# A latent-attention block on one core: four more products in three rounded passes, inverse square roots by one GpSimd power

## The reference

```
x = x + xattn(layernorm(x), ctx)      # q and k are normalised per head of 16 numbers, then softmax(q k) v
x = x + attn(layernorm(x))            # scores = QK/4 + lambda * (tanh(Q) J) tanh(K), causal
h = layernorm(x)
x = x + shared(h) + sum over the two best experts of prob * expert(h)
# shared(h) = (silu(h @ gate) * (h @ up)) @ down ;  router = softmax(h @ router_w)
```

## Time and profile before

| | us |
|---|---|
| median of 3 runs | 1395.9 |
| profiled execution | 1382.5 |
| its span, first to last instruction | 1380.7 |
| TensorE busy in the span (matmuls) | 1240.6 (90%) |
| VectorE busy | 984.4 (71%) |
| ScalarE busy | 698.1 (51%) |
| GpSimd busy | 450.4 (33%) |

### The profile page before, as it was taken

The page is one execution under the profiler, slowest core; times in us unless marked ns, Lnnn a source line. Parts: engine busy times, 40 slices in busy tenths (PEclk is TensorE's granted clock), DMA queues, the critical chain, the costliest instruction groups (busy, mean ns, idle before and its releaser), DMA issues.

```text
span 1380.7 us, 54869 instructions
## 1 busy us (share of the span) xinstructions
PE 1240.6 (90%) x22808; PEld 1024.0 (74%) x22808; DVE 984.4 (71%) x2498; ACT 698.1 (51%) x1377; POOL 450.4 (33%) x436
## 2 busy tenths in 40 slices
PE   3789999999999999999999999999999986699950
PEld 3677878888888878788878787888888864488840
DVE  7458777777777777777777777777777763365547
ACT  1345555555555555555555555555555542255520
POOL 1322333333333333333333333333333222155530
PEclk7789999999999999999999999999999998699985
DMA  4100111111111111103111100111111002586558
GB/s 155 39 21 4 48 49 49 49 49 49 49 49 51 56 44 51 34 30 100 33 34 33 36 29 28 34 33 34 34 38 33 15 14 63 157 245 188 163 188 262
DMA packets 82579, 92.12 MB, mean 67 GB/s; under 512 B 17248, under 2 KB 72544, under 8 KB 82016
## 3 DMA queue, kind: packets, MB, share of 16 engines
q1 hardware_dynamic: 70816, 65.41, 16.4%
q0 software_dynamic: 6912, 19.01, 3.8%
q10 hardware_dynamic: 4608, 4.20, 0.9%
HBM read 61.19 MB, written 33.78 MB: 69 GB/s over the span
## 4 chain that ended last, share of the span: by engine, by line
PE 82%; DVE 9%; issue 4%; DMA 2%; ACT 1%; POOL 1%; SPq 0%; DVEq 0%; POOLq 0%; ACTq 0%
PE ringB L489 16%; PE ringC L500 14%; PE oA L582 10%; PE banksS L565 9%; DVE mx L1220 6%; PE banksS L783 5%; PE banksS L529 4%; PE ringB L663 3%; PE ringB L617 2%; PE ringB L649 2%; PE banksS L634 2%; PE ringB L484 2%; DMA out<-ksq 2%; PE oA L489 2%; PE banksS L544 2%
## 5 line engine op out<-in xcount | busy, mean ns | idle before, releaser
L863 ACT ACTIVATE pt<-banksS 128x1024 f32<-128x1024 f32 x128 | 127.7, 1023 | 129.6 <-PE banksS L565 118.0
L1039 POOL TENSOR_TENSOR kn<-kc,rr 128x512 f32<-128x512 f32 x64 | 66.6, 1062 | 336.0 <-DVE rr L1208 336.0
L500 PE MATMUL ringC<-wx_kv,ct 128*128 128x256 f32 x512 | 159.9, 312 | 13.6 <-DVE ws_down L1362 6.2
L1220 DVE TENSOR_REDUCE mx<-banksS 128x8 f32<-128x2048 f32 x64 | 146.3, 2287 | 0.9 <-PE banksS L544 0.9
L500 PE MATMUL ringC<-wx_kv_rest,ct 128*128 128x256 f32 x512 | 146.8, 287 | 0.0
L500 PE MATMUL ringC<-wx_kv,ct_rest 128*128 128x256 f32 x512 | 146.0, 285 | 0.0
L1033 POOL TENSOR_TENSOR sc<-sc,rz 128x1024 f32<-128x1024 f32 x32 | 62.3, 1948 | 223.5 <-DVE rz L1281 223.5
L565 PE MATMUL banksS<-qT,kT 17*128 17x64 f32 x4096 | 132.4, 278 | 0.9 <-DVE qT L1225 0.9
L565 PEld LDWEIGHTS banksS<-qT,kT 17*128 17x128 f32 x4096 | 123.5, 191 | 7.9 <-issue 1.4
L500 PEld LDWEIGHTS ringC<-wx_kv,ct 128*128 128x128 f32 x512 | 99.3, 194 | 27.6 <-DVE pos_u L1338 7.8
L1234 DVE RECIPROCAL rz<-oA 128x128 f32<-128x128 f32 x64 | 61.3, 957 | 55.5 <-PE oA L582 55.5
(11 more groups left out here) (219 smaller groups left out, 2957.0 us busy)
## 6 DMA issues: line engine op xcount, KB each, us to landing
ct_in<-in_ctxT SPq DMA_DIRECT2D x64, 256.0 KB, 3.1
pt<-rows_by_expert SPq DMA_DIRECT2D x80, 130.0 KB, 2.4
rows_by_expert<-in_pad_rows SPq DMA_DIRECT2D x16, 260.0 KB
xt<-in_x SPq DMA_DIRECT2D x32, 128.0 KB, 3.5
rows_without_experts<-base SPq DMA_DIRECT2D x32, 128.0 KB
pt<-expert_rows SPq DMA_DIRECT2D x16, 256.0 KB, 4.1
kn<-expert_rows SPq DMA_DIRECT2D x16, 256.0 KB, 4.2
out<-ksq ACTq DMA_DIRECT2D x32, 128.0 KB, 3.8
```

The lines of the kernel that those rows point to most:

```text
L500: mm = pe.matmul(ringC[:, half * DIM:(half + 1) * DIM], left[:, p, k, j // 2, (j % 2) * P:(j % 2 + 1) * P], right[:, k, part * DIM:(part + ...
L863: act.activation(pt[:, g, :, :, :, :].rearrange("p i q c n -> p i (q c n)"), banksS[:, :, g * 256:(g + 1) * 256], ACT.Exp)\
L1039: pool.tensor_tensor(kn[:, 2 * jj:2 * jj + 2, :, 0:HD].rearrange("p j h d -> p (j h) d"), kc[:, 2 * jj:2 * jj + 2, :].rearrange("p j (h d) ...
L1220: dve.tensor_reduce(mx[:, 2 * r:2 * r + 2, :, HD].rearrange("p q i -> p i q"), banksS[:, :, :].rearrange("p i (q m) -> p i q m", q=2), AX. ...
```

## The change

1. QK, VP, ROUTE and GU become `split_product`: six rounded passes for each. ScalarE's copies of x1T and hT now round (`rounded["NT"]`, `rounded["HT"]`), and VectorE subtracts the rounded rows from the bank to get the rest (`self_rows_rest`, `ffn_rows_rest`), which is also what frees the bank. The weights are loaded into buffers that self attention uses later (sc, qkn, qk4) and are split on VectorE once, in step 3, where the scaling of jmix and ws_down now stands too (before: step 2).
2. The first guess and the Newton steps go; VectorE only makes mean plus epsilon (`mean_squares`), and GpSimd raises 80 columns to the power -0.5 in front of the key scaling.
3. Orders: TensorE turns x1n in front of rough_scores 0 instead of behind it; VectorE's keys 0 stand at the end of a step instead of the start of the next, ScalarE's probs_in 1 likewise; the two subtractions get places.
4. Room: w_down gets no buffer of its own but lies over kn and kT; its four loads are issued after the last tile's C1, its scaling stands in step 36 instead of 34, the w_gu loads come in steps 6 to 13, and the last pass uses other buffers.

```diff
+            def split_product(bank_, u, t, left, left_rest, source, right, right_rest, n):
+                pe.wait_ge(rounded[source].sem, rounded[source].of(t))
+                for r in (right, right_rest):
+                    for k in range(KD):
+                        pe.matmul(bank_[:, 0:n], left[:, k, :], r[:, k, 0:n], start=(r is right and k == 0), stop=False)
+                pe.wait_ge(free[source].sem, free[source].of(t))
+                for k in range(KD):
+                    mm = pe.matmul(bank_[:, 0:n], left_rest[:, k, :], right[:, k, 0:n], start=False, stop=(k == 1))
+                mm.then_inc(full[u].sem, 1)
...
             def self_qk(b, p):
                 if b == 0:
                     pe.wait_ge(self_weights_in, 16 * 7)
+                    pe.wait_ge(weights_set, 2)
                 claim(pe, B_USES, B_BANKS, "QK", b)
-                pe.wait_ge(free["NT"].sem, free["NT"].of(b))
-                product(bankB("QK"), "QK", lambda k: x1T[:, k, :], wa_qk, 2 * DIM)
+                split_product(bankB("QK"), "QK", b, x1T, x1T_rest, "NT", wa_qk, wa_qk_rest, 2 * DIM)
...
             def step(s, odd):
+                on(s, odd, 4, self_rows_turned)
                 on(s, odd, 3, rough_scores, 0)
-                on(s, odd, 4, self_rows_turned)
...
+            def inverse_sigmas(c, p):
+                pool.wait_ge(ev["s_eps"].sem, ev["s_eps"].of(c))
+                freed(pool, ev["qn_ready"], c)
+                pool.tensor_tensor(rr[:, :], ss[:, :], minushalf[:, :].to_broadcast([P, 5 * H]), ALU.pow).then_inc(ev["sigmas_ready"].sem, 1)
...
-            def inverse_sigmas(a, p):
+            def mean_squares(a, p):
 
                 for s in ("q_sum", "k_sum0", "k_sum1"):
                     dve.wait_ge(ev[s].sem, ev[s].of(a))
                 dve.tensor_scalar(ss[:, :], ss[:, :], 1.0 / HD, EPS, ALU.mult, ALU.add).then_inc(ev["s_eps"].sem, 1)
...
-                for n in range(3):
...
+            def self_rows_rest(b, p):
+                dve.wait_ge(rounded["NT"].sem, rounded["NT"].of(b))
+                freed(dve, full["QK"], b)
+                freed(dve, full["VP"], b)
+                dve.tensor_tensor(x1T_rest[:, :, :].rearrange("p k n -> p (k n)"), bankB("NT")[:, 0:DIM],
+                                  x1T[:, :, :].rearrange("p k n -> p (k n)").bitcast(F32), ALU.subtract).then_inc(free["NT"].sem, 1)
...
             def step(s, odd):
-                if s == TILES + 2:
+                if s == TILES + 4:
                     dve.wait_ge(expert_weights_in, 16 * 12)
                     dve.tensor_scalar(w_down[:, :, :], w_down[:, :, :], 0.5, None, ALU.mult).then_inc(weights_set, 1)
-                if s == 2:
+                if s == 3:
                     dve.wait_ge(self_weights_in, 16 * 7)
+                    split = ((wa_qk, wa_qk_rest, wa_qk_in), (wa_v, wa_v_rest, wa_v_in), (ws_gu, ws_gu_rest, ws_gu_in), (w_route, w_route_rest, w_route_in))
+                    for whole, _, source in split:
+                        ins = dve.tensor_copy(whole[:, :, :], source)
+                    ins.then_inc(setup_dve, 1)
+                    dve.wait_ge(setup_dve, 9)
+                    for whole, rest, source in split:
+                        dve.tensor_tensor(rest[:, :, :], source, whole[:, :, :].bitcast(F32), ALU.subtract)
                     dve.tensor_scalar(jmix[:, :, :], jmix[:, :, :], cols[:, 4:5], None, ALU.mult)
                     dve.tensor_scalar(ws_down[:, :, :], ws_down[:, :, :], 0.5, None, ALU.mult).then_inc(weights_set, 1)
-                on(s, odd, 2, keys, 0)
+                on(s, odd, 4, self_rows_rest)
                 on(s, odd, 3, maxima, 0)
...
                 on(s, odd, 2, key_sums, 1)
+                on(s, odd, 5, ffn_rows_rest)
                 on(s, odd, 2, queries)
...
+                on(s, odd, 1, keys, 0)
...
+                if s == TILES + 2:
+                    sp.wait_ge(full["C1"].sem, full["C1"].of(TILES - 1))
+                    for piece in range(4):
+                        load_expert_weights(piece)
```

More of the change, by code:

```diff
@@ L125, in perceiver_block @@
         w_gu = sb("w_gu", [P, KD, E, 2 * F])
-        w_down = sb("w_down", [P, E, DIM])
         wmean = sb("wmean", [P, KD, 3 * H])
@@ L163, in perceiver_block @@
         x1b = sb("x1b", [P, DIM])
-        x1T = sb("x1T", [P, KD, P])
+        x1T, x1T_rest = (sb(n, [P, KD, P], F32R) for n in ("x1T", "x1T_rest"))
         qkn = sb("qkn", [P, 2, H, PAD])
@@ L180, in perceiver_block @@
         h = sb("h", [P, 2, 2, ROW])
-        hT = sb("hT", [P, KD, P])
+        hT, hT_rest = (sb(n, [P, KD, P], F32R) for n in ("hT", "hT_rest"))
         th = sb("th", [P, DIM])
@@ L224, in perceiver_block @@
                    qn[:, :, :].rearrange("p h d -> p (h d)"), v2[:, :, :, :].rearrange("p h o d -> p (h o d)"),
[L225 removed]
+                   qm[:, :, :].rearrange("p q n -> p (q n)"), wa_o[:, :, :].rearrange("p k d -> p (k d)"),
+                   jmix[:, :, :].rearrange("p q n -> p (q n)"), ws_down[:, :, :].rearrange("p k d -> p (k d)"), xt[:, :], xn[:, :])
         bases = [t[:, k * DIM:(k + 1) * DIM] for t in resting for k in range(t.shape[1] // DIM)]
         rows_d = nc.dram_tensor("rows_by_expert", (E * ROOM + E * P, ROW), F32, kind="Internal").ap()
+        wa_qk_in = sc[:, :, :].rearrange("p a n -> p (a n)").rearrange("p (k n) -> p k n", k=KD)
+        ws_gu_in = qkn[:, :, :, :].rearrange("p i h d -> p i (h d)")
+        wa_v_in = qk4[:, 0, :, :].rearrange("p q n -> p (q n)").rearrange("p (k n) -> p k n", k=KD)
+        w_route_in = qk4[:, 1, 0, 0:KD * E].rearrange("p (k n) -> p k n", k=KD)
         base_d = nc.dram_tensor("rows_without_experts", (TOK, DIM), F32, kind="Internal").ap()
@@ L261, in claim @@
                 back -= banks
+        rounded = {}
+        for u in ("NT", "HT"):
+            rounded[u], free[u] = Event(free[u].sem, 1, 2), Event(free[u].sem, 2, 2)
         x1_ready, x2_ready, su_ready = free["X1"], free["WO"], free["GU"]
@@ L285, in perceiver_block @@
             ev.update(chain(f"{ln}_norm", f"{ln}_stats", f"{ln}_meanvar", f"{ln}_veps"))
-        ev.update(chain("newton", "s_eps", "s_shift", "newton_y0", *(f"newton_{s}" for n in range(3)
-                        for s in (f"t{n}", f"u{n}", f"y{n + 1}"))))
+        ev.update(chain("s_eps", "s_eps"))
+        ev.update(chain("sigmas", "sigmas_ready", "kn1_ready", "kn0_ready"))
         ev.update(chain("weights_b0", "weights0", "weights1"))
@@ L372, in load_self_weights @@
             def load_self_weights():
-                for dst, name in ((wa_qk, "wa_qk"), (wa_v, "wa_v"), (w_route, "w_route"), (ws_down, "ws_down")):
-                    load(dst[:, :, :], halves(name), self_weights_in)
-                load(ws_gu[:, :, 0:DIM], halves("ws_gate"), self_weights_in)
-                load(ws_gu[:, :, DIM:2 * DIM], halves("ws_up"), self_weights_in)
+                for dst, name in ((wa_qk_in, "wa_qk"), (wa_v_in, "wa_v"), (w_route_in, "w_route"), (ws_down[:, :, :], "ws_down")):
+                    load(dst, halves(name), self_weights_in)
+                load(ws_gu_in[:, :, 0:DIM], halves("ws_gate"), self_weights_in)
+                load(ws_gu_in[:, :, DIM:2 * DIM], halves("ws_up"), self_weights_in)
                 load(jmix[:, :, :], w["jmix"], self_weights_in)
@@ L640, in self_values @@
                 pe.wait_ge(free["NT"].sem, free["NT"].of(b))
-                product(bankB("VP"), "VP", lambda k: x1T[:, k, :], wa_v)
+                split_product(bankB("VP"), "VP", b, x1T, x1T_rest, "NT", wa_v, wa_v_rest, DIM)
             def probs_turned(b, p, g):
@@ L680, in route @@
                 claim(pe, B_USES, B_BANKS, "RT", d)
-                pe.wait_ge(free["HT"].sem, free["HT"].of(d))
-                product(bankB("RT"), "RT", lambda k: hT[:, k, :], w_route, E)
+                split_product(bankB("RT"), "RT", d, hT, hT_rest, "HT", w_route, w_route_rest, E)
             def counts(d, p):
@@ L696, in gate_and_up @@
                 claim(pe, B_USES, B_BANKS, "GU", d)
-                pe.wait_ge(free["HT"].sem, free["HT"].of(d))
-                product(bankB("GU"), "GU", lambda k: hT[:, k, :], ws_gu, 2 * DIM)
+                split_product(bankB("GU"), "GU", d, hT, hT_rest, "HT", ws_gu, ws_gu_rest, 2 * DIM)
             def gated_turned(d, p):
```

65 lines of the change are left out of this document (30 added, 35 removed).

## The result

The changed kernel takes 1591.8 us (median of four runs, 1590.9 to 1599.8) against 1395.2 for the kernel before on the same chip: a ratio of 1.142, 95% interval 1.140 to 1.145. It is slower by 197 us, where 1388 had been forecast. In the medians and ratios of this document, executions more than 1.5% above the fastest of their kernel are set aside (four of the ten of experiment 1, one in each of four others). The profiled execution has a span of 1589.1 us, before 1380.7.

What follows compares the result with a forecast made beforehand. TensorE's instruction issue time, tile after tile, with the short waits between, was taken as the bound. Products -24.0, stall +9.3 and ramp +7.0 gave -7.7 us: 1374.8 profiled, 1388 median; range 1374 to 1402, leaving out a long power.

Steps and rivals of the forecast that it cites:

- X: Duration of GpSimd's one power over 80 columns, in place of Newton's steps: taken as 4.0 us, bounds 0.5 and 12.4.
- the power is long: Rival: power on GpSimd between s_eps and KT outlasts its cover; at 12.4 us the kernel takes 1490 us; chance 0.12.
- The threshold of 9.3 us: Steady tiles, before KT: a power up to 9.3 us is hidden; each us above costs a us per tile.
- The four products: QK, GU, VP and ROUTE on TensorE as six rounded passes each: -0.775 us per tile, -24.0 us over 31 tiles.
- The stall at O1: Second half of self_weighted waits for the x1T subtraction to free bank 0: 0.30 us per tile, +9.3 us in all.
- nothing is lost: Turning x1n (NT) ahead of rough_scores 0 costs nothing, since O0 waits for the second pT copy anyway.
- The VectorE queue behind the subtraction: Maxima 0 to maxima 1 on VectorE: maxima 0 starts 0.83 us later, but qkn and maxima 1 start 0.1 earlier.
- the wait at MT: TensorE's 0.28 us wait for the VectorE maxima in a tile's opening stretch: claimed to stay what it was.
- The ramp: Start of the kernel: +1.1 for tile 0, -0.7 step 2, +5.6 weight splitting, +1.0 clock, together +7.0 us.
- bf16 pace: Rival: rounded weights load as fast as bf16 ones, 98 against 194 ns, 11 us less, 1377 us; chance 0.02.
- The drain: End of the kernel: later w_down loads and halving, and the last step's ROUTE and GU, change nothing: 0.
- the gain is eaten in front: Rival: 512-column pass takes 0.235 us, or VectorE's queue to maxima 1 is 0.3 late; 1396 us; chance 0.20.

Runs made afterwards that it cites:

- experiment 1: Changed kernel with the inverse square roots back on VectorE by shift and three Newton steps, everything else as changed: 1397.8 us, ratio 1.0002 to the kernel before.
- 48 columns: Changed kernel with the GpSimd power over 48 of the 80 columns and Newton's steps on VectorE for the other 32: 1419.9 us, ratio 1.019.
- with 64: Changed kernel with the power over 64 columns, Newton for 16: 1519.5 us, ratio 1.088; with the query scaling moved ahead of the self-attention sums: 1486.3 us, 1.067.
- experiment 6: Experiment 1's kernel, weight split moved behind the inverse square roots, plus ScalarE's first probability eviction (pT) ahead of both query evictions: 1396.4 us, ratio 1.002.
- power alone (2): Kernel before with only Newton's steps replaced by one GpSimd power over 80 columns, ahead of the key scaling: 1571.0 us, ratio 1.127.
- rough scores first (8): Experiment 7's kernel with TensorE's rough scores put back ahead of the turning of the self-attention rows: 1400.3 us, ratio 1.003.
- QK and VP single (8): Experiment 7's kernel with QK and VP back as single full-precision products, without x1T's remainder, only GU split: 1385.4 us, ratio 0.993.
- experiment 7: Experiment 6's kernel with ROUTE back as one full-precision product, VectorE making the rounded hT copy: 1374.3 us, ratio 0.987; repeated on another chip 1372.1 us, 0.987.

## Why the prediction was wrong

**The failed step is the value chosen for X, the power's duration.** It was bounded between 0.5 and 12.4 us, and 4.0 was taken, "nearer the lower row", because the 0.15 us that the one-column power costs above the fixed part holds the start of a loop as well. Mostly it doesn't. With 1, 48, 64 and 80 columns the durations are 0.54, 8.03, 10.55 and 13.13 us: 0.16 us for every column. The upper row was right, and even 5% short. The row that was the same operation with another width should have outweighed the rows of another operation with about the same width. The rival "the power is long" had the place, the mechanism and a threshold; it got 0.12.

**What the rival itself missed.** A us above the threshold was to cost a us; 1490 was its time, 1592 came. Above 9.3 us lie 3.8; the tile in the profile pays 4.23 of wait and 2.47 of lower clock, 1.75 us per us. Tile 0 was to pay -2.9 + 13.1 = 10.2 and paid 12.1 (136.89 against 124.78 in experiment 1).

**The threshold of 9.3 us** is about right for TensorE's wait: at 8.03 us it doesn't wait for the keys, at 10.55 it does (14 times, 22.6 us). It isn't a threshold of the time, though: 48 columns cost 22 us more than none, and with 64 a queue behind the power that had been checked for its due time alone (context rest and self_probs) held a VectorE instruction by running beside it. The prediction named who is queued behind the power and asked only when they are due, not what they meet.

**The four products**, forecast -0.775 us a tile. By the starts of all matmuls, experiment 1 against the kernel before: QK with the product ahead of it -0.32 (forecast -0.43), GU -0.28 (-0.43; -0.32 in tiles without a fall of the clock), VP -0.17 (-0.15), ROUTE +0.22 (+0.24), together -0.55. ROUTE and VP are right, so the weight load does set the pace at 256 columns and below. The 512-column pass is the mis-sized term: GU's middle pair in the tile above lasts from 715.15 to 715.62, 0.235 us a pass, where 0.213 was taken and 0.235 was the worst case. Half of the unrounded pass was the wrong row again; twice the rounded 256-column one was the right one. Rounded weights don't load at the bf16 pace (ROUTE's pass takes 0.115 us), so here too the trace speaks against the rule of the Trainium skill ("TensorE: Matmul & The Clock Gate", Weight-path perf modes), if the rounded type counts as one other than FP32.

**The stall at O1**, forecast 0.30, between 0 and 0.55: from their start at 701.96 to the next product the 64 matmuls take 1.29 us, in the kernel before 1.11 in the mean, so 0.18 in the changed kernel. The step was right and over-sized, but "nothing is lost" for the turning in its new place was not: it waits some 0.2 us for the pT eviction behind the last key product, which experiment 6 removed. Together they are 0.4 us a tile. The VectorE queue behind the subtraction did what was said: the wait at MT is 0.28 as before.

**The ramp**, without the power forecast +5.9: 124.78 - 119.58 = 5.2 by experiment 1. The block splitting the weights took 5.5 us of VectorE (forecast 5.6) and cost 3.2. **The drain**, forecast 0: +1.5 after.

**What the sum left out** is the clock in the steady stretch. -0.55 a tile comes to -17 us, the two waits give +12, the ramp +5: by this sum experiment 1 should be even, and it is (1.0002). But the sum was read from two profiled executions, and all the executions together show another way to the same time. Span times mean granted clock estimates what an execution would take at full clock; the rest of the span is what the lower clock costs (the profiled execution of experiment 1: 1396.7 x 0.946 = 1321, and 76). Against the kernel before on the same chip, in us, means of all executions counted:

| | executions | at full clock | by the clock |
|---|---|---|---|
| power alone (2) | 4 | +94 | +83 |
| Newton back (1) | 6 | -8 | +9 |
| pT first (6) | 12 | -17 | +21 |
| routing unsplit (7) | 6 | -26 | +9 |
| rough scores first (8) | 11 | -10 | +13 |
| QK and VP single (8) | 11 | -16 | +6 |

By this estimate the gain is there in the mean, 8 us where the forecast's sum without the power comes to 8.8, and the clock takes it back: every kernel with split products runs at a lower mean clock than the kernel before. The two profiled executions don't show the gain (1321 us at full clock against 1318), so its size is less certain than the clock's part. The eviction order of experiment 6 gave its expected 5 to 8 us too, and again the clock took them. So "the gain is eaten in front" was right for the part without the power in its time (1396) and only in part in its reason, the pass width; that it came out is partly luck. What makes the clock fall in a stretch with the same short waits stays open.

## What to carry to other kernels

When an operation isn't in the trace, price it by the row of the same operation at another size before any row of another operation at the same size; and where the two bounds lie on both sides of the slack, the choice between them is the forecast. A product split into rounded ones pays where its columns set the pace (512 and 256 here) and loses where the weight load does (16): split only the former. Here that, with the eviction order of experiment 6, turned 1.00 into 0.987. Count the remainder as well: QK's and VP's faster passes were nearly all paid back by the stall that their remainder causes. For work moved to GpSimd ask of each instruction queued behind it not only when it is due but which VectorE instruction it will now run beside; 0.1 us decided over 1.5. And compare tiles by their mean: one tile with an idle moment made an expectation wrong here.

## What the runs showed of the hardware

A power costs GpSimd 0.16 us per column of 128 partitions, 13.13 us for 80, where an addition takes 0.73 us for 256; Newton's eleven VectorE instructions for all 80 took 2.9 us. A VectorE operation with both inputs in SBUF took 4.19 us instead of 0.36, until two GpSimd operations on SBUF had ended, and 2.08 us where a GpSimd operation had started 0.1 us before it. The granted clock of TensorE fell to half and cost 1.7 us at a time, also in stretches without an idle moment; the profile of experiment 6 had twelve such falls in its steady stretch, two executions of one kernel (experiment 7) had four and eleven, and that of the kernel with the rough scores first, where TensorE waits 0.43 us more in every tile, had none.
